# Query, key and value projections as three fp16 products of a split input, transposed by transfers

## The chip, the cores and the metric

The kernel runs on one NeuronCore of a Trainium2 chip. Its engines are TensorE (PE, matmuls, whose weight loads are listed as PEld), VectorE (DVE), ScalarE (ACT), GpSimd (POOL) and SyncE (SP, which here only issues transfers). The metric is the device time of one execution in microseconds (us); lower is better.

## The reference

Four layers with residuals over `x` of 32 items, 256 tokens, width 128: an attention with biases, a mixture of experts, an attention without biases, the mixture again. Cut to the part that matters:

```
x = x + attention_a(layernorm(x), Wq, bq, Wk, bk, Wv, bv, Wo)   # 16 heads of 8
x = x + ffn(layernorm(x), ...)
x = x + attention_b(layernorm(x), w_qkv, w_out)                  # 16 heads of 8
x = x + ffn(layernorm(x), ...)
# attention: q, k, v = xn @ Wq, xn @ Wk, xn @ Wv; softmax(q k^T) v; @ Wo
```

All of it is in fp32.

## The kernel before

The 32 items pass twice through one pipeline, once for each attention with the mixture behind it, as 64 turns. The program of each engine is a loop over steps n = -6 to 70 and, inside, over eight places p = 0 to 7; an engine does its instructions in exactly that order and waits for the others by semaphores. In step n TensorE works on several turns at once: the scores of turn n+2 for their maxima (`max_side`, L840, read by VectorE's `nmax`, L643), the scores of turn n again for the exponentials (`exp_side`, L850, read by ScalarE, L717), the weighted sums of turn n (`weigh`, L829), and at single places the small products of a turn's way in and out, which all go through one bank of PSUM, `m_bank`. `fill_m` lets each of these wait until the one before it has been read.

The way in of a turn is this. In step n VectorE takes the statistics of turn n+6. GpSimd normalises turn n+5 into `xy[.][:, 0]`, and turn n-3, behind its attention, into `xy[.][:, 1]` (L537). At p=6 TensorE transposes both, four 128x128 pieces (L1010), and ScalarE copies the first pair to `xnT` (L794) and the second to `normT` (L797). At p=2 of the next step the query and key projections read `xnT` (L816 from `by_columns`: eight fp32 matmuls of 32 columns of weights each; the trace counts two instructions for each fp32 matmul). ScalarE adds the biases and writes `qk32` (L753 and L754; in the second attention one copy, L756). GpSimd splits `qk32` into two fp16 parts (L550, L553), SP stores the parts to DRAM (`scratch`, six transfers, L431) and loads them back as `q_stack` and `k_stack` (L414) at its next step, once those stores have landed. At p=5 the value projection reads `xnT` too (L816), and ScalarE copies it to `values` (L781).

SP's order in a step is: wait for the stores of the step before to land, and for the exponentials' matmuls; issue the two loads; wait for `maxT` (the maxima, L724); issue its two transfers (L420); wait for the parts; issue the six stores. GpSimd's order is: the maxima (L515 to L519, which TensorE transposes at p=1, L950), the normalisation, the weights of the experts for one or two turns, the parts.

At p=3 TensorE transposes `oT` (L977), which shares `m_bank` and so waits until ScalarE has read the query and key product. After the query and key product at p=2 only one `exp_side`, one `max_side` and one more `exp_side` come before that.

In the opening, ScalarE and VectorE find the norms of the projections' weights and scale query and key weights against each other by powers of two, before the first projection.

Of the kernel before, what the change touches and what calls it, by code (L numbers as in the profile page):

```python
# [34 lines left out]
COARSE = 32768.0  # L35

# [25 lines left out]
def build(nc, x_dram_in, attn_w, attn_b, gate_w, down_w, down_b, up_w, up_b, tail_c, ident_c, iota_c, pick_c, out):  # L62
    ctx = ExitStack()
    with ctx:
# [19 lines left out]
        xnT = [sb(f"xnT{i}", [P, TOKENS]) for i in range(2)]  # L84
# [15 lines left out]
        bks = sb("bks", [P, 1])  # L100
        ident = sb("ident", [P, P])
        identh = sb("identh", [P, P], FP16)
        ones = sb("ones", [P, P])
        norms = sb("norms", [P, 4])
        norms_b = sb("norms_b", [P, 2])
        total = sb("total", [P, 2, 2])
        inverse = sb("inverse", [P, 2])
        ratio = sb("ratio", [P, 2])
        quarter = sb("quarter", [P, 2], U32)
        exponent = sb("exponent", [P, 2, 2], U32)  # L110
        factor = sb("factor", [P, 2, 2])
# [89 lines left out]
        def scalar_opening(act):  # L201
# [26 lines left out]
        def vector_opening(dve):  # L228
# [11 lines left out]
            dve.wait_ge(squares_done, 4)  # L240
            then(nc.vector.tensor_tensor(norms[:, 0:2], norms[:, 0:2], norms_b[:, :], ALU.add))
            assert done[0] == NORMS_READY
            dve.wait_ge(norms_summed, 1)
            then(nc.vector.tensor_scalar(total[:, :, :].rearrange("p a b -> p (a b)"), m_bank[:, 0:4], 1.0, 1e-30, ALU.mult, ALU.add))
            assert done[0] == TOTAL_READ
            then(nc.vector.reciprocal(inverse[:, :], total[:, :, 0]))
            then(nc.vector.tensor_tensor(ratio[:, :], total[:, :, 1], inverse[:, :], ALU.mult))
            then(nc.vector.tensor_scalar(quarter[:, :], ratio[:, :].bitcast(U32), 25, None, ALU.logical_shift_right))
            then(nc.vector.tensor_scalar(exponent[:, 0, :], quarter[:, :], 1.0, 96.0, ALU.mult, ALU.add))
            then(nc.vector.tensor_scalar(exponent[:, 1, :], quarter[:, :], -1.0, 158.0, ALU.mult, ALU.add))  # L250
            then(nc.vector.tensor_scalar(factor[:, :, :].bitcast(U32), exponent[:, :, :], 23, None, ALU.logical_shift_left))
            to_q, to_q_b = float(HEAD) ** -0.5, float(WIDTH) ** -0.5
            nc.vector.tensor_scalar(wa[:, 0:WIDTH], wa[:, 0:WIDTH], factor[:, 0, 0:1], to_q, ALU.mult, ALU.mult)
            nc.vector.tensor_scalar(wa[:, WIDTH:2 * WIDTH], wa[:, WIDTH:2 * WIDTH], factor[:, 1, 0:1], None, ALU.mult)
            nc.vector.tensor_scalar(bqs[:, :], wa[:, 4 * WIDTH:4 * WIDTH + 1], factor[:, 0, 0:1], to_q, ALU.mult, ALU.mult)
            nc.vector.tensor_scalar(bks[:, :], wa[:, 4 * WIDTH + 1:4 * WIDTH + 2], factor[:, 1, 0:1], None, ALU.mult)
            nc.vector.tensor_scalar(wb[:, 0:WIDTH], wb[:, 0:WIDTH], factor[:, 0, 1:2], to_q_b, ALU.mult, ALU.mult)
            nc.vector.tensor_scalar(wb[:, WIDTH:2 * WIDTH], wb[:, WIDTH:2 * WIDTH], factor[:, 1, 1:2], None, ALU.mult).then_inc(weights_ready, 1)  # L258
            dve.wait_ge(weights_ready, 1)

        def tensor_opening(pe):
            pe.wait_ge(balancing, NORMS_READY)
            nc.tensor.matmul(m_bank[:, 0:4], ones[:, :], norms[:, :], start=True, stop=True).then_inc(norms_summed, 1)
            m_reader[0] = (balancing, TOTAL_READ)
# [42 lines left out]
        def live(turn):  # L307

            return 0 <= turn < TURNS

        projections = [[w[:, i * WIDTH:(i + 1) * WIDTH] for i in range(4)] for w in (wa, wb)]
# [767 lines left out]
```

## Time and profile before

| | |
|---|---|
| time, median of 3 runs | 932.47 us (931.51 to 935.1) |
| the profiled execution: its own time | 931.88 us |
| its span, first to last instruction | 930.1 us |
| busy, PE | 861.5 us, 93% of the span |
| busy, DVE | 781.5 us, 84% |
| busy, ACT | 757.5 us, 81% |
| busy, POOL | 539.8 us, 58% |
| queue of SP: bytes, share of 16 transfer engines | 69.52 MB, 24.8% |

The profiled execution is 0.6 us below the median of the runs, and 1.8 us of it lie outside the span. The busy shares are means over an opening of about 50 us, a steady stretch to about 850 us and an ending.

### The profile page before, as it was taken

The page shows a single profiled execution, that of the slowest core. Times are in us where ns is not written, and L with a number is a line of the kernel's source. Part 1 is how long each engine was busy: PE and PEld are TensorE (multiplying, and loading weights), DVE is VectorE, ACT ScalarE, POOL GpSimd, SP SyncE. Part 2 cuts the span into 40 slices and gives each one's busy share as a digit, 9 for nine tenths or more (in the row PEclk, how much of TensorE's full clock was granted, in tenths as well). Part 3 has the DMA queues.
Part 4 walks back from the last instruction along what each step waited for, and adds up shares of the span by engine and source line. Part 5 has one row for each costly group of instructions (what it writes and reads, how often), then busy time and mean ns, then how long its engine had stood idle before and what let it go on. Part 6 is the DMA issues. An engine that isn't in the chain of part 4 may idle for free.

```text
span 930.1 us, 32135 instructions
## 1 busy us (share of the span) xinstructions
PE 861.5 (93%) x12592; PEld 444.0 (48%) x12592; DVE 781.5 (84%) x1410; ACT 757.5 (81%) x1305; POOL 539.8 (58%) x1086
## 2 busy tenths in 40 slices
PE   3699999999999999999999999999999999998875
PEld 1244444444445454455545445455554554554434
DVE  2889999999998989989898998989889888889533
ACT  2278888888888888888988898888898888897864
POOL 7345555545664766647565674657576485653432
PEclk9989999999999999999999999999999999999987
DMA  3354233222222222212222221222223133132001
GB/s 107 119 159 142 79 89 102 83 74 67 78 78 76 60 80 68 83 50 80 78 72 70 66 83 58 83 66 82 59 71 99 47 102 95 54 104 64 4 24 46
DMA packets 89862, 72.16 MB, mean 78 GB/s; under 512 B 5040, under 2 KB 72784, under 8 KB 89680
## 3 DMA queue, kind: packets, MB, share of 16 engines
q1 hardware_dynamic: 89280, 69.52, 24.8%
q8 instruction: 101, 1.65, 0.8%
q10 hardware_dynamic: 432, 0.59, 0.2%
q14 instruction: 49, 0.40, 0.1%
HBM read 39.68 MB, written 29.88 MB: 75 GB/s over the span
## 4 chain that ended last, share of the span: by engine, by line
PE 66%; DVE 18%; issue 8%; ACT 4%; POOL 2%; DMA 1%; POOLq 0%; SPq 0%; DVEq 0%; ACTq 0%
PE values_bank L829 19%; DVE nmax L643 14%; PE ring L840 11%; PE ring L850 10%; PE m_bank L816 9%; PE m_bank L977 4%; PE m_bank L1010 3%; PE ring L880 3%; PE ring L903 3%; ACT probs L717 2%; PE m_bank L950 1%; PE ring L895 1%; DMA wb<-in_attn_b 0%; DVE x L631 0%; DVE x L678 0%
## 5 line engine op out<-in xcount | busy, mean ns | idle before, releaser
L643 DVE TENSOR_REDUCE nmax<-ring 128x4 f32<-128x1024 f32 x512 | 603.7, 1216 | 46.6 <-PE ring L840 44.5
L717 ACT ACTIVATE probs<-ring 128x1024 f32<-128x1024 f32 x512 | 520.7, 1034 | 35.6 <-PE ring L850 32.9
L829 PE MATMUL values_bank<-probs,values 128*32 128x256 f32 x4096 | 277.0, 384 | 1.7 <-ACT probs L717 1.7
L850 PE MATMUL ring<-q_stack,k_stack 32*128 32x256 f16 x2048 | 198.4, 273 | 14.1 <-DVE nmax L643 14.0
L537 POOL TENSOR_SCALAR xy<-x,mv,rstd 128x128 f32<-128x128 f32 x256 | 201.7, 798 | 7.9
L840 PE MATMUL ring<-k_stack,q_stack 32*128 32x256 f16 x2048 | 183.2, 277 | 15.3 <-DMA k_stack<-scratch 5.1
L515 POOL TENSOR_SCALAR mparts<-nmax 128x32 f16<-128x32 f32 x64 | 14.1, 220 | 279.1 <-DVE nmax L643 279.0
L829 PEld LDWEIGHTS values_bank<-probs,values 128*32 128x32 f32 x4096 | 123.9, 109 | 63.8 <-issue 23.8
L850 PEld LDWEIGHTS ring<-q_stack,k_stack 32*128 32x128 f16 x2048 | 64.4, 92 | 132.7 <-issue 73.7
L840 PEld LDWEIGHTS ring<-k_stack,q_stack 32*128 32x128 f16 x2048 | 52.9, 93 | 115.4 <-ACT probs L717 41.2
L781 ACT COPY values<-m_bank 128x128 f32<-128x128 f32 x128 | 28.9, 278 | 60.3 <-PE m_bank L816 59.0
L553 POOL TENSOR_TENSOR parts<-qk,parts 128x512 f16<-128x512 f32 x64 | 74.3, 1160 | 5.3
L530 POOL TENSOR_TENSOR rstd<-varp,minus_half 128x4 f32<-128x4 f32 (+1 forms) x72 | 69.6, 967 | 6.0
L572 DVE BATCH_NORM_STATS2 raw<-x 128x6 f32<-128x128 f32 x256 | 60.9, 280 | 3.7 <-DMA x<-in_x 3.7
L631 DVE TENSOR_TENSOR x<-x,m_bank 128x256 f32<-128x256 f32 x64 | 27.0, 421 | 40.2 <-PE m_bank L816 40.2
L1010 PE MATMUL m_bank<-ident,xy 128*128 128x128 f32 x256 | 45.0, 294 | 5.4 <-ACT qk L754 1.0
L744 ACT COPY oT<-values_bank 128x512 f32<-128x512 f32 x64 | 37.6, 587 | 15.3 <-PE values_bank L829 15.3
L550 POOL TENSOR_SCALAR parts<-qk 128x512 f16<-128x512 f32 x64 | 39.7, 621 | 14.6 <-ACT qk L754 13.1
L678 DVE TENSOR_TENSOR x<-x,ring 128x512 f32<-128x512 f32 x32 | 22.0, 688 | 30.0 <-PE ring L903 30.0
L977 PE MATMUL m_bank<-ident,oT 128*128 128x128 f32 x256 | 41.9, 286 | 2.4 <-ACT oT L744 1.3
L816 PE MATMUL m_bank<-xnT,wa 128*32 128x256 f32 x512 | 38.6, 424 | 2.4 <-DVE wb L258 1.8
L482 POOL COPY wu<-up_sb 64x128 f32 x112 | 32.7, 292 | 11.8 <-POOL wd L476 9.1
(118 smaller groups left out, 959.7 us busy)
## 6 DMA issues: line engine op xcount, KB each, us to landing
scratch<-parts SPq DMA_DIRECT2D x384, 64.0 KB
q_stack<-scratch SPq DMA_DIRECT2D x64, 256.0 KB, 2.6
k_stack<-scratch SPq DMA_DIRECT2D x64, 256.0 KB, 3.0
out<-x SPq DMA_DIRECT2D x16, 256.0 KB, 3.0
x<-in_x SPq DMA_DIRECT2D x3, 768.0 KB, 6.5
q_stack<-maxT SPq DMA_DIRECT2D x128, 8.0 KB
x<-in_x SPq DMA_DIRECT2D x1, 896.0 KB, 6.7
x<-in_x SPq DMA_DIRECT2D x1, 640.0 KB, 5.3
```

Of the source, the lines that this page charges most:

```text
L530: nc.gpsimd.tensor_tensor(rstd[i][:, both, :], varp[i][:, both, :], minus_half[:, both, :], ALU.pow).then_inc(rstd_done, 1)
L537: last = nc.gpsimd.tensor_scalar(xy[i][:, m, t, :], x[:, (turn % ITEMS) * TILES + t, :], mv[i][:, m, t, 0:1], rstd[i][:, m, t:t + 1], ALU. ...
L553: nc.gpsimd.tensor_tensor(parts[i][:, 1], qk32[i][:, :, :], parts[i][:, 0], ALU.subtract).then_inc(parts_ready, 1)
L572: last = nc.vector.bn_stats(raw[i][:, t, :], x[:, (turn % ITEMS) * TILES + t, :])
L643: nc.vector.tensor_reduce(dst, src, axis=AX.X, op=ALU.max, negate=True).then_inc(max_done, 1)
L717: nc.scalar.activation(probs[g % 2][:, c:c + 2, :, :], pair_of("exps", n, p)[:, :, :].rearrange("p x (k q) -> p x k q", k=TILES), ACT.Exp) ...
L816: last = nc.tensor.matmul(out[at], stationary[:, at], moving, start=start, stop=stop, skip_group_check=True)
L829: last = nc.tensor.matmul(values_bank[32 * c:32 * (c + 1), a * TOKENS:(a + 1) * TOKENS], values[turn % RING][:, k, PER_GROUP * g + c, :], ...
L840: last = nc.tensor.matmul(pair_of("scores", turn, p)[:, a, t * TOKENS:(t + 1) * TOKENS], q_stack[z][rows, p // 2, t * P:(t + 1) * P], k_st ...
L850: last = nc.tensor.matmul(pair_of("exps", turn, p)[:, a, k * TOKENS:(k + 1) * TOKENS], k_stack[r][rows, of // 2, k * P:(k + 1) * P], q_sta ...
L977: last = nc.tensor.transpose(m_bank[:, at:at + P], oT[(n - 1) % 2][:, a, t * P:(t + 1) * P], ident[:, :])
L1010: last = nc.tensor.transpose(m_bank[:, at:at + P], xy[(n + 5) % 2][:, m, t, :], ident[:, :])
```

## The change

GpSimd writes the normalised turn n+5, scaled up by 2^8, as two fp16 parts into `xn` (a rounding and a rest, two more instructions). SP transposes them by four transfers of 128x128 into `xnT`, which now has four buffers of two fp16 parts each, at a place between the transfers of `maxT` and the stores of the parts. TensorE no longer transposes that half of `xy`, and ScalarE no longer copies it. The weights are split once, in the opening, into two fp16 parts (`w_parts`), after scaling by powers of two that now cover the value weights and their output weights too. Query, key and value projections become three fp16 products each (`PRODUCTS`: first by first, first by second, second by first part), with weights of 128 columns: per turn, query and key take 6 matmuls of 256 columns, and value 6 of 128, in place of 8 and 8 of `by_columns`. ScalarE undoes the scaling by a `scale` of its copies. The output projection stays as it was.

```diff
+PRODUCTS = ((0, 0), (0, 1), (1, 0))
...
-        xnT = [sb(f"xnT{i}", [P, TOKENS]) for i in range(2)]
+        xn = [sb(f"xn{i}", [P, 2, TILES, WIDTH], FP16) for i in range(2)]
+        xnT = [sb(f"xnT{i}", [P, 2, TOKENS], FP16) for i in range(RING)]
+        w_parts = [sb(f"w_parts{i}", [P, 2, 3 * WIDTH], FP16) for i in range(2)]
...
-            for c, w in enumerate((wa[:, 0:WIDTH], wa[:, WIDTH:2 * WIDTH], wb[:, 0:WIDTH], wb[:, WIDTH:2 * WIDTH])):
-                last = nc.scalar.activation(onT[:, 0:WIDTH], w, ACT.Square, scale=float(WIDTH) ** 0.5, accum_out=norms[:, c:c + 1])
+            for c, w in enumerate(m[:, i * WIDTH:(i + 1) * WIDTH] for m in (wa, wb) for i in range(3)):
+                last = nc.scalar.activation(onT[:, 0:WIDTH], w, ACT.Square, scale=float(WIDTH) ** 0.5, accum_out=norms[:, c // 3, c % 3:c % 3 + 1])
...
+            to_q = (float(HEAD) ** -0.5, float(WIDTH) ** -0.5)
+            for b, w in enumerate((wa, wb)):
+                nc.vector.tensor_scalar(w[:, 0:WIDTH], w[:, 0:WIDTH], factor[:, b, 0:1], to_q[b], ALU.mult, ALU.mult)
+                for i in (1, 2):
+                    last = nc.vector.tensor_scalar(w[:, i * WIDTH:(i + 1) * WIDTH], w[:, i * WIDTH:(i + 1) * WIDTH], factor[:, b, i:i + 1], None, ALU.mult)
+                if b == 0:
+                    nc.vector.tensor_scalar(bqs[:, :], wa[:, 4 * WIDTH:4 * WIDTH + 1], factor[:, 0, BIAS_Q:BIAS_Q + 1], to_q[0], ALU.mult, ALU.mult)
+                    nc.vector.tensor_scalar(bks[:, :], wa[:, 4 * WIDTH + 1:4 * WIDTH + 2], factor[:, 0, BIAS_K:BIAS_K + 1], None, ALU.mult)
+                    nc.vector.tensor_scalar(bvs[:, :], wa[:, 4 * WIDTH + 2:4 * WIDTH + 3], factor[:, 0, BIAS_V:BIAS_V + 1], None, ALU.mult)
+                then(nc.vector.tensor_scalar(w[:, 3 * WIDTH:4 * WIDTH], w[:, 3 * WIDTH:4 * WIDTH], factor[:, b, BACK_V:BACK_V + 1], None, ALU.mult))
+                then(nc.vector.tensor_copy(w_parts[b][:, 0, :], w[:, 0:3 * WIDTH]))
+                nc.vector.tensor_tensor(w_parts[b][:, 1, :], w[:, 0:3 * WIDTH], w_parts[b][:, 0, :], ALU.subtract).then_inc(weights_ready, 1)
+                dve.wait_ge(weights_ready, b + 1)
...
+                    if live(n + 5):
+
+                        sp.wait_ge(xn_ready, (n + 5) + 1)
+                        if live(n + 1):
+                            sp.wait_ge(v_done, (n + 1) + 1)
+                        for part in range(2):
+                            for t in range(TILES):
+                                sp.dma_start(xnT[(n + 5) % RING][:, part, t * P:(t + 1) * P], xn[(n + 5) % 2][:, part, t, :],
+                                             transpose=True).then_inc(xnT_in[(n + 5) % 2], 16)
...
-                        if norm_steps(n) > 2:
-                            pool.wait_ge(xyT_done, norm_steps(n - 2))
+                        if live(n - 5):
+                            pool.wait_ge(yT_done, (n - 5) + 1)
                         for m, turn in ((0, n + 5), (1, n - 3)):
                             for t in range(TILES):
                                 if live(turn):
                                     last = nc.gpsimd.tensor_scalar(xy[i][:, m, t, :], x[:, (turn % ITEMS) * TILES + t, :], mv[i][:, m, t, 0:1],
                                                                    rstd[i][:, m, t:t + 1], ALU.subtract, ALU.mult)
                         last.then_inc(xy_ready, 1)
+                        if live(n + 5):
+                            if live(n + 3):
+                                pool.wait_ge(xnT_in[(n + 3) % 2], (n + 3) // 2 * 64 + 64)
+                            pool.wait_ge(xy_ready, norm_steps(n))
+                            nc.gpsimd.tensor_scalar(xn[i][:, 0, :, :], xy[i][:, 0, :, :], 1.0, 0.0, ALU.mult, ALU.add).then_inc(xhi_done, 1)
+                            pool.wait_ge(xhi_done, (n + 5) + 1)
+                            nc.gpsimd.tensor_tensor(xn[i][:, 1, :, :], xy[i][:, 0, :, :], xn[i][:, 0, :, :], ALU.subtract).then_inc(xn_ready, 1)
...
+                        same = factor[:, (n + 4) // ITEMS, SAME:SAME + 1]
                         if n + 4 < ITEMS:
-                            nc.scalar.activation(qk32[i][:, 0, :], src[:, 0, :], ACT.Identity, bias=bqs[:, :])
-                            last = nc.scalar.activation(qk32[i][:, 1, :], src[:, 1, :], ACT.Identity, bias=bks[:, :])
+                            nc.scalar.activation(qk32[i][:, 0, :], src[:, 0, :], ACT.Identity, bias=bqs[:, :], scale=same)
+                            last = nc.scalar.activation(qk32[i][:, 1, :], src[:, 1, :], ACT.Identity, bias=bks[:, :], scale=same)
                         else:
-                            last = nc.scalar.copy(qk32[i][:, :, :], src)
+                            last = nc.scalar.activation(qk32[i][:, :, :], src, ACT.Copy, scale=same)
                         last.then_inc(qk32_ready, 1)
...
-                    if p == 5 and (live(n + 5) or live(n - 3)):
-                        act.wait_ge(xyT_done, norm_steps(n))
-                        if live(n + 5):
-                            nc.scalar.copy(xnT[(n + 5) % 2][:, :], m_bank[:, 0:TOKENS]).then_inc(xnT_ready, 1)
-                        if live(n - 3):
-                            item = (n - 3) % ITEMS
-                            nc.scalar.activation(normT[:, item:item + 1, :], m_bank[:, TOKENS:2 * TOKENS].unsqueeze(1), ACT.Copy,
-                                                 accum_out=pooled[:, item:item + 1]).then_inc(yT_ready, 1)
+                    if p == 5 and live(n - 3):
+                        act.wait_ge(yT_done, (n - 3) + 1)
+                        item = (n - 3) % ITEMS
+                        nc.scalar.activation(normT[:, item:item + 1, :], m_bank[:, 0:TOKENS].unsqueeze(1), ACT.Copy, scale=2.0 ** -UP,
+                                             accum_out=pooled[:, item:item + 1]).then_inc(yT_ready, 1)
...
-                        wq, wk = projections[(n + 4) // ITEMS][0:2]
+                        parts_w, parts_x = w_parts[(n + 4) // ITEMS], xnT[(n + 4) % RING]
                         fill_m(pe, qk32_ready, (n + 4) + 1)
-                        if n + 4 == 0:
-                            pe.wait_ge(weights_ready, 1)
-                        pe.wait_ge(xnT_ready, (n + 4) + 1)
-                        for a, wmat in enumerate((wq, wk)):
-                            last = by_columns(m_bank[:, a * TOKENS:(a + 1) * TOKENS], wmat, xnT[(n + 4) % 2][:, :],
-                                              start=(a == 0), stop=(a == 1))
+                        if n + 4 in (0, ITEMS):
+                            pe.wait_ge(weights_ready, (n + 4) // ITEMS + 1)
+                        pe.wait_ge(xnT_in[(n + 4) % 2], (n + 4) // 2 * 64 + 64)
+                        for a in range(2):
+                            for k, (w, h) in enumerate(PRODUCTS):
+                                last = nc.tensor.matmul(m_bank[:, a * TOKENS:(a + 1) * TOKENS], parts_w[:, w, a * WIDTH:(a + 1) * WIDTH], parts_x[:, h, :],
+                                                        start=(a == 0 and k == 0), stop=(a == 1 and k == len(PRODUCTS) - 1), skip_group_check=True)
                         last.then_inc(qk_done, 1)
...
-                        wv = projections[(n + 3) // ITEMS][2]
+                        parts_w, parts_x = w_parts[(n + 3) // ITEMS], xnT[(n + 3) % RING]
                         fill_m(pe, v_ready, (n + 3) + 1)
                         for t in range(TILES):
-                            last = by_columns(m_bank[:, t * P:(t + 1) * P], xnT[(n + 3) % 2][:, t * P:(t + 1) * P], wv,
-                                              start=(t == 0), stop=(t == TILES - 1))
+                            for k, (w, h) in enumerate(PRODUCTS):
+                                last = nc.tensor.matmul(m_bank[:, t * P:(t + 1) * P], parts_x[:, h, t * P:(t + 1) * P], parts_w[:, w, 2 * WIDTH:3 * WIDTH],
+                                                        start=(t == 0 and k == 0), stop=(t == TILES - 1 and k == len(PRODUCTS) - 1), skip_group_check=True)
                         last.then_inc(v_done, 1)
...
-                    if p == 6 and (live(n + 5) or live(n - 3)):
-                        fill_m(pe, *((yT_ready, (n - 3) + 1) if live(n - 3) else (xnT_ready, (n + 5) + 1)))
+                    if p == 6 and live(n - 3):
+                        fill_m(pe, yT_ready, (n - 3) + 1)
                         pe.wait_ge(xy_ready, norm_steps(n))
-                        for m in range(0 if live(n + 5) else 1, 2 if live(n - 3) else 1):
-                            for t in range(TILES):
-                                at = (m * TILES + t) * P
-                                last = nc.tensor.transpose(m_bank[:, at:at + P], xy[(n + 5) % 2][:, m, t, :], ident[:, :])
-                        last.then_inc(xyT_done, 1)
+                        for t in range(TILES):
+                            last = nc.tensor.transpose(m_bank[:, t * P:(t + 1) * P], xy[(n + 5) % 2][:, 1, t, :], ident[:, :])
+                        last.then_inc(yT_done, 1)
```

On SP, in a plain step of the first attention, the row of transfers before was this (the names in brackets are the semaphores that an issue waits for: `bounced` the stores' landing, `t_done` the exponentials' matmuls, `hi_ready` and `parts_ready` the two parts of `qk32`).

```order
L414 DMA q_stack<-scratch 128x1024 [waits t_done,bounced1]
L414 DMA k_stack<-scratch 128x1024
L420 DMA q_stack<-maxT 4x4x256 [waits maxT_ready]
L420 DMA q_stack<-maxT 4x4x256
L431 DMA scratch<-parts 4x32x256 [waits hi_ready,stack_in0]
L431 DMA scratch<-parts 4x32x256 x3
L431 DMA scratch<-parts 4x32x256 [waits parts_ready]
L431 DMA scratch<-parts 4x32x256
```

Now it is this, at the same place.

```order
L433 DMA q_stack<-scratch 128x1024 [waits t_done,bounced0]
L433 DMA k_stack<-scratch 128x1024
L439 DMA q_stack<-maxT 4x4x256 [waits maxT_ready]
L439 DMA q_stack<-maxT 4x4x256
L447 DMA_TRANSPOSE xnT<-xn 128x128 [waits v_done,xn_ready]
L447 DMA_TRANSPOSE xnT<-xn 128x128 x3
L459 DMA scratch<-parts 4x32x256 [waits hi_ready,stack_in1]
L459 DMA scratch<-parts 4x32x256 x3
L459 DMA scratch<-parts 4x32x256 [waits parts_ready]
L459 DMA scratch<-parts 4x32x256
```

Four transposing transfers and a wait for `xn_ready` stand ahead of the stores; nothing else moved.

On PE, from the query and key product (p=2) to the transposes of `oT` (p=3), a plain step before reads so.

```order
L816 MATMUL m_bank<-xnT,wa 32x256 x8
L850 MATMUL ring<-q_stack,k_stack 128x256 x4
L840 MATMUL ring<-k_stack,q_stack 128x256 x4
L850 MATMUL ring<-q_stack,k_stack 128x256 x4
L977 MATMUL m_bank<-ident,oT 128x128 x4
```

Now:

```order
L998 MATMUL m_bank<-xnT,w_parts 128x256 x6
L883 MATMUL ring<-q_stack,k_stack 128x256 x4
L873 MATMUL ring<-k_stack,q_stack 128x256 x4
L883 MATMUL ring<-q_stack,k_stack 128x256 x4
L1011 MATMUL m_bank<-ident,oT 128x128 x4
```

Six fp16 matmuls stand for eight fp32 ones; what follows is the same.

On PE at p=5 and p=6, from the value product to the transposes of `xy`, before:

```order
L816 MATMUL m_bank<-wa,xnT 32x128 x8
L829 MATMUL values_bank<-probs,values 32x256 x8
L1000 MATMUL m_bank<-ident,o 128x128 x2
L850 MATMUL ring<-q_stack,k_stack 128x256 x4
L840 MATMUL ring<-k_stack,q_stack 128x256 x4
L1010 MATMUL m_bank<-ident,xy 128x128 x4
```

and now:

```order
L1024 MATMUL m_bank<-w_parts,xnT 128x128 x6
L862 MATMUL values_bank<-probs,values 32x256 x8
L1035 MATMUL m_bank<-ident,o 128x128 x2
L883 MATMUL ring<-q_stack,k_stack 128x256 x4
L873 MATMUL ring<-k_stack,q_stack 128x256 x4
L1043 MATMUL m_bank<-ident,xy 128x128 x2
```

Two of the four transposes are gone, and the value product has six matmuls.

## Rows read from the trace of the kernel before

**Rows 1.** Windows, steady stretch: busy us (count) of PE, PEld, DVE, ACT, POOL; clock; DMA share; GB/s.

```profile
50.00:850.00 800.00, 774.88 (x11682) 398.43 (x11676) 714.43 (x1249) 692.25 (x1178) 481.97 (x947) 1.00 0.27 80
```

**Rows 2.** Chain that ended last, 560 to 586 us, second attention: start, us, what.

```profile
561.93 0.22 PE ring L895 x2
...
574.46 1.23 DVE nmax L643
...
576.12 0.59 PE m_bank L1010 x4
...
581.38 1.00 PE m_bank L816 x16
```

**Rows 3.** The same chain, 300 to 326 us, first attention.

```profile
313.57 0.30 ACT oT L744
...
315.33 0.49 ACT qk L754
...
315.87 0.66 PE m_bank L977 x4
```

**Rows 4.** Timeline of SP's issues, 300 to 328 us: start, us, line, transfer, count.

```profile
306.62 3.44 SPq L431 DMA_DIRECT2D scratch<-parts  x6
312.87 0.33 SPq L414 DMA_DIRECT2D q_stack<-scratch  x1
...
313.72 1.16 SPq L420 DMA_DIRECT2D q_stack<-maxT  x2
318.50 3.46 SPq L431 DMA_DIRECT2D scratch<-parts  x6
324.89 0.33 SPq L414 DMA_DIRECT2D q_stack<-scratch  x1
```

**Rows 5.** Timeline of PE, 564 to 590 us: start, us, line, tiles, shapes, count.

```profile
573.42 0.64 PE L816 MATMUL m_bank<-wb,xnT 128*32 128x128 f32 x16
573.88 1.05 PE L829 MATMUL values_bank<-probs,values 128*32 128x256 f32 x16
574.86 0.44 PE L1000 MATMUL m_bank<-ident,o 128*128 128x128 f32 x2
575.23 0.39 PE L850 MATMUL ring<-q_stack,k_stack 32*128 32x256 f16 x4
575.73 0.39 PE L840 MATMUL ring<-k_stack,q_stack 32*128 32x256 f16 x4
...
583.33 0.66 PE L977 MATMUL m_bank<-ident,oT 128*128 128x128 f32 x4
```

**Rows 6.** Timeline of ACT, 564 to 590 us.

```profile
582.53 0.59 ACT L756 COPY qk<-m_bank 128x512 f32<-128x512 f32 x1
```

**Rows 7.** The page's costliest groups: the split of `qk32` on POOL, mean ns after the comma.

```profile
L553 POOL TENSOR_TENSOR parts<-qk,parts 128x512 f16<-128x512 f32 x64 | 74.3, 1160 | 5.3
...
L550 POOL TENSOR_SCALAR parts<-qk 128x512 f16<-128x512 f32 x64 | 39.7, 621 | 14.6 <-ACT qk L754 13.1
```

**Rows 8.** Timeline of POOL, a step's first instruction; in brackets its idle time before.

```profile
180.10 0.22 POOL L515 TENSOR_SCALAR mparts<-nmax 128x32 f16<-128x32 f32 x1 [4.89 <-DVE nmax L643]
431.32 0.22 POOL L515 TENSOR_SCALAR mparts<-nmax 128x32 f16<-128x32 f32 x1 [1.40 <-DVE nmax L643]
443.41 0.22 POOL L515 TENSOR_SCALAR mparts<-nmax 128x32 f16<-128x32 f32 x1 [3.13 <-DVE nmax L643]
...
756.66 0.22 POOL L515 TENSOR_SCALAR mparts<-nmax 128x32 f16<-128x32 f32 x1
```

**Rows 9.** Chain that ended last, the opening.

```profile
5.97 0.41 ACT onT L208 x2
...
11.12 0.23 DVE wb L258
...
11.45 1.97 PE m_bank L816 x16
```

**Rows 10.** Timeline of PE, 300 to 328 us: the next step's query and key product.

```profile
325.99 1.07 PE L816 MATMUL m_bank<-xnT,wa 128*32 128x256 f32 x16
```

More of the change, by code:

```diff
@@ L103, in build @@
         ones = sb("ones", [P, P])
-        norms = sb("norms", [P, 4])
+        norms = sb("norms", [P, 2, 3])
         norms_b = sb("norms_b", [P, 2])
[L106 to L111, printed above, removed]
+        total = sb("total", [P, 2, 3])
+        quarter = sb("quarter", [P, 2, 3], U32)
+        level = sb("level", [P, 2, 3])
+        both_of = sb("both_of", [P, 2, 2])
+        exponent = sb("exponent", [P, 2, 8], U32)
+        factor = sb("factor", [P, 2, 8])
         minus_half = sb("minus_half", [P, 2, TILES])
@@ L245, in vector_opening @@
             assert done[0] == TOTAL_READ
[L246 to L250, printed above, removed]
@@ L256, in vector_opening @@
[L256 to L259, printed above, removed]
+            then(nc.vector.tensor_scalar(quarter[:, :, :], total[:, :, :].bitcast(U32), 25, None, ALU.logical_shift_right))
@@ new lines, in vector_opening @@
+            then(nc.vector.tensor_scalar(level[:, :, :], quarter[:, :, :], 1.0, 0.0, ALU.mult, ALU.add))
+            nc.vector.tensor_tensor(both_of[:, :, 0], level[:, :, 0], level[:, :, 1], ALU.add)
+            then(nc.vector.tensor_tensor(both_of[:, :, 1], level[:, :, 1], level[:, :, 0], ALU.subtract))
+            bias = 127.0
+            nc.vector.tensor_scalar(exponent[:, :, 0:3], level[:, :, :], -2.0, bias + TO_TARGET, ALU.mult, ALU.add)
+            nc.vector.tensor_scalar(exponent[:, :, SAME], both_of[:, :, 0], 1.0, bias - UP - TO_TARGET, ALU.mult, ALU.add)
@@ new lines, in vector_opening @@
+            nc.vector.tensor_scalar(exponent[:, :, BIAS_Q], both_of[:, :, 1], 1.0, bias, ALU.mult, ALU.add)
+            nc.vector.tensor_scalar(exponent[:, :, BIAS_K], both_of[:, :, 1], -1.0, bias, ALU.mult, ALU.add)
+            nc.vector.tensor_scalar(exponent[:, :, BIAS_V], level[:, :, 2], -2.0, bias + UP + TO_TARGET, ALU.mult, ALU.add)
+            then(nc.vector.tensor_scalar(exponent[:, :, BACK_V], level[:, :, 2], 2.0, bias - UP - TO_TARGET, ALU.mult, ALU.add))
+            then(nc.vector.tensor_scalar(factor[:, :, :].bitcast(U32), exponent[:, :, :], 23, None, ALU.logical_shift_left))
@@ L261, in tensor_opening @@
         def tensor_opening(pe):
             pe.wait_ge(balancing, NORMS_READY)
[L263 removed]
+            nc.tensor.matmul(m_bank[:, 0:6], ones[:, :], norms[:, :, :].rearrange("p a b -> p (a b)"), start=True, stop=True).then_inc(norms_summed, 1)
             m_reader[0] = (balancing, TOTAL_READ)
@@ L309, in live @@
             return 0 <= turn < TURNS
-        projections = [[w[:, i * WIDTH:(i + 1) * WIDTH] for i in range(4)] for w in (wa, wb)]
+        out_weights = [w[:, 3 * WIDTH:4 * WIDTH] for w in (wa, wb)]
         raw_done, raw2_done, mv_done, mv2_done = sem("raw_done"), sem("raw2_done"), sem("mv_done"), sem("mv2_done")
         var_done, rstd_done, xy_ready = sem("var_done"), sem("rstd_done"), sem("xy_ready")
-        xyT_done, xnT_ready, yT_ready = sem("xyT_done"), sem("xnT_ready"), sem("yT_ready")
+        xhi_done, xn_ready = sem("xhi_done"), sem("xn_ready")
+        xnT_in = [sem(f"xnT_in{i}") for i in range(2)]
+        yT_done, yT_ready = sem("yT_done"), sem("yT_ready")
         qk_done, qk32_ready = sem("qk_done"), sem("qk32_ready")
@@ L786, in step @@
                         if n - 1 < ITEMS:
-                            last = nc.scalar.activation(onT[:, :], m_bank[:, 0:TOKENS], ACT.Identity, bias=wa[:, 514:515])
+                            last = nc.scalar.activation(onT[:, :], m_bank[:, 0:TOKENS], ACT.Identity, bias=bvs[:, :])
                         else:
```

17 lines of the change are left out of this document (8 added, 9 removed).

## The prediction

> **What bounds the kernel now.** I read the busy time of the steady stretch first, then the chain that ended last inside one step of each attention, and then the queue that the change loads, SP's. From 50 to 850 us TensorE is busy 774.88 of 800 us at full granted clock (1.00), VectorE 714.43, ScalarE 692.25 and GpSimd 481.97 [rows 1]. So TensorE is the bound, but VectorE and ScalarE are within 8% and 11% of it, and a gain on TensorE soon meets one of them. The chain shows where. In a step of the second attention it runs through TensorE except for one stretch: a maximum of 1.23 us on VectorE that ends where TensorE goes on towards the transposes of `xy`, whose four pieces cost 0.59 us there; the query and key product costs 1.00 us [rows 2]. In the first attention it leaves TensorE a second time: from 313.57 it runs through ScalarE (the copy of `oT`, an exponential, the two biased copies of `qk32`, the last from 315.33 for 0.49 us) and returns at 315.87 with the transposes of `oT` [rows 3]. There TensorE waits for ScalarE, so a shorter product ahead of it wins nothing.
>
> SP works in a closed loop, since its first wait in a step is for the stores of the step before to land. The six stores take 3.46 us to issue, end at 321.96, and the loads start at 324.89, 2.93 us later; from the first load to `maxT` it is 0.85 us, and `maxT` takes 1.16 us [rows 4]. That is 3.46 + 2.93 + 0.85 + 1.16 = 8.40 us which SP needs for a step, whatever the others do.
>
> **The change, part by part: TensorE.** Two of four transposes at p=6 go. Two such pieces elsewhere (L1000) take 575.23 - 574.86 = 0.37 us from start to start [rows 5], four 0.59 [rows 2], so 0.22 us is saved, on the chain in both attentions. (Both ends: 0.15, if the first pieces carry most of the cost, and half, 0.30.) The steps that do this under a busy TensorE are n = 0 to 58: 59 x 0.22 = 13.0 us.
>
> Query and key become six 16-bit matmuls of 256 columns. A pair of such matmuls (L895, bf16) costs 0.22 us on the chain [rows 2], so six cost 0.66 against 1.00: 0.34 us less. In the first attention I count none of it, as ScalarE ends last there [rows 3]. In the second, ScalarE's copy ends at 582.53 + 0.59 = 583.12 [rows 6] and the transposes of `oT` start at 583.33 [rows 5], so 0.21 us can be won before ScalarE ends last there too: 32 x 0.21 = 6.7 us. The ends are 0 and 0.34.
>
> The value product takes 573.88 - 573.42 = 0.46 us; then TensorE reaches an `exp_side` of four at 575.23, which takes 0.39 us, and the next `max_side` starts only at 575.73 [rows 5], when VectorE releases it [rows 2]. Six matmuls of 128 columns cost between half of 0.11 each (0.33 us) and all of it (0.66). A gain is lost in that wait of 0.11 us; a loss of 0.20 would pass it by 0.09, 5 us over 59 steps. I count zero.
>
> **ScalarE and GpSimd.** ScalarE loses the copy to `xnT`, which is on neither chain: zero. GpSimd gains two instructions of 256 columns. Their kinds at 512 columns take 0.62 and 1.16 us [rows 7]; halves are 0.31 and 0.58, the whole is the other end; with a fixed part and the gaps I take 1.2 us a step (0.9 to 1.8). GpSimd idles 3.13 us before the first instruction of a plain step (4.89 early on); a plain step is 443.41 - 431.32 = 12.09 us [rows 8]. A step shorter by 0.43 and work longer by 1.2 leave 1.5 us. That cover is thin where GpSimd splits the experts' biases, 1.40 us at 431.32, and gone where it has also prepared two turns, at 756.66 [rows 8]. There the maxima's parts come late, behind them their transposes at p=1, and all of TensorE behind these. The batches' table gives seven such splits up to n = 58: six times 0.2 and once 1.6 are 2.8 us, of which I take 2, as TensorE asks a little after the parts are due (0 to 8).
>
> **Opening.** Before the first product ScalarE squares six weights in place of four, 0.43 us each (0.41 and the gap); VectorE does about five more scalings of numbers and four more of weights or biases at some 0.2 us (the last one before took 0.23), less two that now come later, and two splits of 384 columns, an estimated 0.45 each; the first product, 1.97 us at the opening's clock, becomes some 0.45 shorter [rows 9]. That is 0.86 + 1.0 + 0.4 + 0.9 - 0.45, about 2.5 us later for all that follows (0 to 5).
>
> **SP and the four transfers.** They must fit twice. First, into the loop: a step of 12.09 - 0.43 = 11.66 us leaves 11.66 - 8.40 = 3.26 us, or 0.82 us for each; at (12.09 - 8.40) / 4 = 0.92 us the loop alone makes a step as long as before. No row shows a transposing transfer. Issues cost SP from 0.33 us (one load) to 0.58 (`maxT` 1.16 / 2, a store 3.46 / 6) [rows 4]; the far end is 2.93 us, if each had to land before the next. I take 0.58: `maxT` is the row that also goes from SBUF to SBUF. 4 x 0.58 = 2.3 us fit, with 1 us to spare. Second, by the time of use: GpSimd finishes `xn` before the parts, whose first store goes out at 318.50; so it is ready by 318.50 + 1.2 - 0.62 = 319.1, issued by 321.4, landed (2.93) by 324.3, and the product that reads it starts at 325.99 [rows 4, 10], or 0.43 earlier: 1.3 us to spare. What is queued behind them on SP are the stores, whose loads are wanted only a step later. So the transfers cost zero, as long as an issue stays under 0.82 us.
>
> Here the Trainium skill speaks against the change: the page "VectorE: DVE Perf Modes", section "The three transpose paths", gives 390 ns for a 128x128 piece of 2-byte elements on TensorE and 1309 ns by a transfer, and advises TensorE where PSUM will do as the destination. No run so far shows it. If 1.31 us were what a piece holds SP, the loop would be 8.40 + 5.24 = 13.6 us and the time, an estimate from that page, 931.9 + 59 x 1.55 + 2.5 = 1026 us.
>
> **Sum.** 13.0 + 6.7 - 2.0 - 2.5 = 15.2 us less than the profiled execution's 931.9: 916.7. The median of the runs lies 0.6 above that execution, so 917 us.
>
> **Rivals.** (a) *SP's queue becomes the bound*, the other sign. It decides from 0.92 us an issue. For it: the loop has only 3.7 us of room, a transposing issue is a different instruction, and the skill's page above points that way. Against it: no issue of a comparable shape takes over 0.58. At twice the price of a store, 1.15 us, the loop is 13.0 us, 0.91 over 12.09. 59 x 0.91 + 2.5 gives 988 us, less where steps with an expert group are longer and leave room. At 2.93 us an issue the loop would be 20.1 us.
>
> (b) *The gain turns into waits*: VectorE (89% busy) and ScalarE (87%) [rows 1] hold TensorE up at other places of the step, and a third of the 19.7 us remains, 6.5, against 2.5 in the opening and GpSimd's 2.8 in full: 931 us, no change. For it speaks rows 3; against it, that the chain of the second attention has only one such stretch.
>
> (c) *The transfers land late, with SP free*: if the transfer engines serve the four one after another at 2.93 us each, the last lands at 319.1 + 11.7 = 330.8, 5.2 us after 325.6. A late product returns by way of the maxima and GpSimd's next normalisation two steps later, so 2.6 us a step, 59 times: 1088 us. Against it: the transfer engines are busy 27% of the time [rows 1].
>
> **How the numbers follow.** My forecast has a chance of 0.50, (a) 0.28, (b) 0.13, (c) 0.09. What a measurement tells from no change here is about 0.5%, 4.7 us. The forecast's own range is 908 (0.30 and 0.34 saved, little lost) to 927, nine tenths of it faster by over 0.5%: 0.45; with a fifth of (b), 0.48 faster. The rest of (b) and the forecast's last tenth give 0.14 within; (a) and (c) 0.38 slower once a little is kept for the edges. The range runs from 908, below which I leave 0.05, to 1000, above which lie most of (c) and the dearer quarter of (a), 0.15.
>
> **What would show it.** Right: SP still waits for the parts each step and each of its transposing issues lasts 0.8 us or less; TensorE has no wait for a transfer at the query and key product; plain steps shorter by about 0.2 us in the first and 0.4 in the second attention; `oT`'s transposes waiting for ScalarE in both. Wrong by (a): no wait of SP for the parts, steps of the length of its loop, long issues. By (c): TensorE idle ahead of the product, released by a transfer. By (b): the transposes and the product shorter as said, steps still 12.1 us. By GpSimd: the first instruction of its step without idle time in plain steps.

## The result

The changed kernel takes 1018.4 us (median of 4 runs, 1017.3 to 1020.2) against 933.3 us for the kernel before on the same chip: ratio 1.091, 95% interval 1.089 to 1.094. That is slower, above the range, and on the side of rival (a). The profiled execution has a span of 1017.5 us.

The page of the changed kernel, busy time and the shares of the chain that ended last:

```profile
PE 854.2 (84%) x11184; PEld 439.9 (43%) x11184; DVE 792.1 (78%) x1424; ACT 752.2 (74%) x1245; POOL 606.6 (60%) x1214
...
SPq 42%; PE 18%; DMA 16%; DVE 8%; POOL 6%; issue 6%; ACT 3%; POOLq 1%; DVEq 0%; ACTq 0%
```

Only GpSimd is busier than before as a share of its time, and the chain no longer lies on TensorE: SP's queue has 42% of it and the landing of transfers 16%. In the steady stretch, the row that answers to [rows 1] has TensorE busy 701 of 800 us in place of 775, all engines down but GpSimd:

```profile
50.00:850.00 800.00, 701.01 (x9390) 355.61 (x9388) 656.63 (x1130) 620.19 (x1007) 495.68 (x965) 0.96 0.29 83
```

SP's timeline of the changed kernel, the same stretch as [rows 4] (start, us, line, transfer, count):

```profile
303.25 3.45 SPq L459 DMA_DIRECT2D scratch<-parts  x6
309.91 0.34 SPq L433 DMA_DIRECT2D q_stack<-scratch  x1
...
310.76 1.17 SPq L439 DMA_DIRECT2D q_stack<-maxT  x2
312.04 5.96 SPq L447 DMA_TRANSPOSE xnT<-xn  x4
318.10 3.46 SPq L459 DMA_DIRECT2D scratch<-parts  x6
324.96 0.34 SPq L433 DMA_DIRECT2D q_stack<-scratch  x1
...
327.09 4.95 SPq L447 DMA_TRANSPOSE xnT<-xn  x4
```

Four transposing issues hold SP for 4.95 to 5.96 us; the old issues cost what they cost before. The stores start the moment the transposes are issued, and the next loads start when the stores have landed: from load to load it is 324.96 - 309.91 = 15.05 us, where a plain step was 12.1. SP's waits and the duration of one transposing issue (minimum, median, maximum in ns):

```profile
SPq L433 <- DMA scratch<-parts: 161.4, 61, 3.6
...
SPq L447 <- POOL xn L574: 14.0, 10, 5.2
```

```profile
L447 SPq DMA_TRANSPOSE xnT<-xn x256: 1094/1232/2417, 9.6 to 913.8; - x128
```

SP's long wait is the landing of its own stores; for GpSimd it hardly waits (14.0 us in all), and for TensorE 3.7 us in all. So it is a loop that SP alone closes. What TensorE sees of it is a wait at the query and key product, and then a second price:

```profile
PE m_bank L998 <- DMA xnT<-xn: 67.3, 35, 6.4
```

Windows of the changed kernel (columns as in [rows 1]; the number behind the counts is the granted clock):

```profile
316.00:319.20 3.20, 0.57 (x13) 0.13 (x8) 2.53 (x4) 1.63 (x3) 3.09 (x5) 0.99 0.06 11
319.20:325.00 5.80, 5.60 (x46) 2.71 (x48) 2.05 (x5) 2.85 (x4) 4.27 (x10) 0.50 0.24 69
```

TensorE had been busy 0.57 of 3.2 us, and was then granted half its clock (1.2 GHz) for the next 5.8 us. The product, 0.75 us from start to start at 304.49, took 1.37 us there.

### The profile page after: what moved, and what is told of

It reads as the page before. It is cut to its first block, busy times and chain, and to the rows that moved or that the text cites. A ratio compares the mean times of both kernels' runs of the same rounds, so it can differ in the third digit from the quotient of the medians.

```text
span 1017.5 us, 29763 instructions
## 1 busy us (share of the span) xinstructions
PE 854.2 (84%) x11184; PEld 439.9 (43%) x11184; DVE 792.1 (78%) x1424; ACT 752.2 (74%) x1245; POOL 606.6 (60%) x1214
## 4 chain that ended last, share of the span: by engine, by line
SPq 42%; PE 18%; DMA 16%; DVE 8%; POOL 6%; issue 6%; ACT 3%; POOLq 1%; DVEq 0%; ACTq 0%
SPq L447 23%; DMA scratch<-parts 14%; SPq L459 11%; PE values_bank L862 5%; DVE nmax L678 5%; SPq L439 4%; SPq L433 4%; POOL xy L565 2%; PE ring L913 2%; PE ring L936 2%; ACT probs L752 2%; PE ring L873 2%; PE ring L883 2%; PE m_bank L1011 1%; DMA xnT<-xn 1%
## 5 line engine op out<-in xcount | busy, mean ns | idle before, releaser
L862 PE MATMUL values_bank<-probs,values 128*32 128x256 f32 x4096 | 289.4, 397 | 1.7 <-ACT probs L752 1.7
L873 PE MATMUL ring<-k_stack,q_stack 32*128 32x256 f16 x2048 | 186.4, 285 | 32.9 <-DMA k_stack<-scratch 15.2
L883 PE MATMUL ring<-q_stack,k_stack 32*128 32x256 f16 x2048 | 199.8, 280 | 14.6 <-DVE nmax L678 13.5
L543 POOL TENSOR_SCALAR mparts<-nmax 128x32 f16<-128x32 f32 x64 | 13.8, 216 | 249.1 <-DVE nmax L678 248.5
L862 PEld LDWEIGHTS values_bank<-probs,values 128*32 128x32 f32 x4096 | 121.8, 112 | 76.0 <-issue 27.1
L883 PEld LDWEIGHTS ring<-q_stack,k_stack 32*128 32x128 f16 x2048 | 68.7, 94 | 120.7 <-issue 63.0
L998 PE MATMUL m_bank<-xnT,w_parts 128*128 128x256 f16 x384 | 60.6, 301 | 67.4 <-DMA xnT<-xn 67.3
L998 PEld LDWEIGHTS m_bank<-xnT,w_parts 128*128 128x128 f16 x384 | 35.5, 104 | 89.0 <-issue 77.0
L1011 PE MATMUL m_bank<-ident,oT 128*128 128x128 f32 x256 | 48.1, 318 | 12.3 <-ACT qk L790 8.9
L789 ACT ACTIVATE qk<-m_bank,bqs,factor 128x256 f32<-128x256 f32 x32 | 18.1, 565 | 54.0 <-PE m_bank L998 54.0
L504 POOL COPY wd<-down_sb 128x64 f32 x128 | 25.8, 236 | 36.3 <-issue 36.3
```

Of the source, the lines that this page charges most:

```text
L862: last = nc.tensor.matmul(values_bank[32 * c:32 * (c + 1), a * TOKENS:(a + 1) * TOKENS], values[turn % RING][:, k, PER_GROUP * g + c, :], ...
L873: last = nc.tensor.matmul(pair_of("scores", turn, p)[:, a, t * TOKENS:(t + 1) * TOKENS], q_stack[z][rows, p // 2, t * P:(t + 1) * P], k_st ...
L883: last = nc.tensor.matmul(pair_of("exps", turn, p)[:, a, k * TOKENS:(k + 1) * TOKENS], k_stack[r][rows, of // 2, k * P:(k + 1) * P], q_sta ...
L998: last = nc.tensor.matmul(m_bank[:, a * TOKENS:(a + 1) * TOKENS], parts_w[:, w, a * WIDTH:(a + 1) * WIDTH], parts_x[:, h, :], start=(a == ...
```

## The experiments

Two theories stood first. **A**: the issue of a transposing transfer costs SP 1.23 us, and the loop of SP's issues sets the step (A2: the price goes by the piece of 128 columns, not by the instruction). **B**: moving or landing the data is what is slow, whatever SP issues. C to H came from the first traces and are told where they are tried. "Kernel 4" is the kernel of experiment 4. Line numbers differ a little from kernel to kernel; the names stay.

**1. One transfer in place of four**, over all 512 columns.

```diff
-for part in range(2):
-    for t in range(TILES):
-        sp.dma_start(xnT[..][:, part, t*P:(t+1)*P], xn[..][:, part, t, :], transpose=True)
+sp.dma_start(xnT[..].rearrange("p a (t c) -> p (a t) c", c=P),
+             xn[..].rearrange("p a t w -> p (a t w)"), transpose=True)
```

> One transposing transfer of 512 columns per turn stands for the four of 128; data, order and waits stay. Theory A, SP's loop is the bound and an issue has its price per instruction: one issue of about 1.2 to 1.7 us takes some 3.5 us from SP's loop, the loop falls below TensorE's 11.7 to 12.1 us a step, about 920 us. A2, the price goes by the pieces moved: issue of about 4.5 to 5 us, about 1010 us. Theory B, the transfers' data phase is late for TensorE: the same data, no change, about 1018 us.

948.4 us (944.0 to 950.4), ratio 1.014, interval 1.010 to 1.018. Its transposing issues and SP's waits:

```profile
L445 SPq DMA_TRANSPOSE xnT<-xn x64: 1201/1228/2557, 9.5 to 837.2; - x64
```

```profile
SPq L445 <- POOL xn L573: 108.5, 55, 5.2
SPq L454 <- POOL parts L584: 75.7, 42, 4.5
```

One issue of four times the data costs the same 1.23 us, so the price is the instruction's, and A2 and B fall. SP waits for GpSimd again. But A had expected 920, and 28 us of that did not come.

**2. Only the first parts transposed**, two transfers a step; the products read the first part where they should read the second, so the rest of `x` is left out. GpSimd still makes both parts.

```diff
-for part in range(2):
+for part in range(1):
...
-parts_x[:, h, :]
+parts_x[:, 0, :]
```

> Only the first parts are transposed, by two transfers; the products with the rest read the first part instead, so the rest of x is left out of the result, with the same number of matmuls and the same work on GpSimd. Theory A: 2 x 1.23 us less in SP's loop, 13.9 to 11.4 us, so TensorE is the bound again, about 925 us, with qk steps 0.2 to 0.4 us under those of before. Theory B: half the wait of TensorE remains, about 970 us. If GpSimd's two more instructions were the cause, no change, 1018 us.

948.4 us (947.0 to 951.4), 1.016 (1.012 to 1.019): halving the issues does the same as merging them, and here too A's 925 is missed, by 23 us.

**3. The transfers of `maxT` ahead of SP's wait for the landing**, four transposes as in the change, and **4. the same with one transfer**.

```diff
 def step(sp, n, p):
+    if live(n + 1):   # wait for maxT_ready, its two transfers
+        ...
     if live(n + 3):   # wait for the landing, two loads
         ...
-    if live(n + 1):
-        ...
     if live(n + 5):   # the transposing transfers
```

> On SP the two transfers of maxT stand ahead of the wait for the stores' landing instead of behind the loads; the four transposing transfers are untouched. Theory A: their 1.2 us fall into the wait for the landing, the loop is 1.2 us shorter in some 55 steps, about 955 us. Theory B (transfers land late by themselves): no change, 1018 us.

> One transfer per turn and maxT ahead of the landing, both. Theory A: 920 us as with one transfer alone, since TensorE is the bound already; with A2 (price by pieces) about 950 us. Theory B: 1018 us.

977.7 us (974.5 to 980.0), 1.046 (1.042 to 1.050), and 946.0 us (944.6 to 946.6), 1.013 (1.010 to 1.016). The third takes work out of the loop without touching the transposing transfers and wins 41 us, which a loop of issues explains and B does not; A had expected 955, 23 us less than measured. The fourth wins 2 us over the first, within the spread of their runs, so SP no longer sets the end there; 920 was missed again.

**5. The transfers alone**: the kernel before, with four transposing transfers a step from a constant tile to tiles that nobody reads.

```diff
+for part in range(2):
+    for t in range(TILES):
+        sp.dma_start(extraT[(n+5) % RING][:, part, t*P:(t+1)*P], extra[:, part, t, :], transpose=True)
```

> The kernel of before with four transposing transfers a step added to SP's queue at the same place, from a constant tile to tiles nobody reads; everything else as before. Theory A: the queue alone makes the loss. Its loop becomes 8.4 + 4 x 1.23 = 13.3 us or a little more, so 1.2 to 1.9 us a step over 12.1: 1000 to 1040 us. Rival F: the transfers cost nothing by themselves and the loss comes from the other edits: 933 us.

1004.1 us (1000.5 to 1010.6), 1.072 (1.069 to 1.076). Nothing else was changed, and 69 us of the loss are there. SP's timeline of this kernel (its traced execution took 1010.6 us, the longest of the four):

```profile
303.85 3.46 SPq L445 DMA_DIRECT2D scratch<-parts  x6
310.46 0.34 SPq L418 DMA_DIRECT2D q_stack<-scratch  x1
...
312.53 4.96 SPq L433 DMA_TRANSPOSE extraT<-extra  x4
317.60 3.96 SPq L445 DMA_DIRECT2D scratch<-parts  x6
324.23 0.34 SPq L418 DMA_DIRECT2D q_stack<-scratch  x1
```

The loop is 324.23 - 310.46 = 13.8 us in this step; the stores end at 321.56, so their landing takes 2.7 us of it (3.2 us in the step before).

**6. The parts transposed on TensorE**: no transposing transfer; four 16-bit transposes at p=6, and ScalarE copies them to `xnT`.

```diff
+for k in range(2 * TILES):
+    nc.tensor.transpose(m_bank.bitcast(FP16)[:, 2*TOKENS + k*P : ...], xn[..][:, k // TILES, k % TILES, :], identh)
...
+nc.scalar.copy(xnT[..], m_bank.bitcast(FP16)[:, 2*TOKENS:4*TOKENS])
```

> The changed kernel with its two parts transposed on TensorE (four 16-bit transposes and one copy by ScalarE to xnT) and no transposing transfer. Theory A with C: SP's loop is as short as before, and what is left are the opening (3 us), GpSimd's longer work at the end (8 us), and some 0.2 us more on TensorE a step, of which the shorter product gives back about as much: 935 to 955 us, near 945. Rival F: something in the three-product form itself costs the bulk, not the queue: over 980 us.

944.7 us (943.3 to 946.6), 1.010 (1.008 to 1.013). So F falls, and without SP's loop and without any transposing transfer the three products are still no gain, though TensorE and ScalarE do these transposes here. Where the remainder lies is read from the start of ScalarE's copy to `maxT`, one a turn (us, in the traces):

| kernel | turn 2 | turn 29 | turn 53 | turn 61 |
|---|---|---|---|---|
| before | 59.36 | 408.49 | 733.56 | 847.57 |
| changed | 72.67 | 465.51 | 812.83 | 934.08 |
| 5, transfers alone | 70.35 | 462.45 | 806.27 | 924.35 |
| 4, one transfer, `maxT` first | 61.72 | 414.40 | 739.73 | 861.66 |
| 8, register loads earlier | 60.31 | 412.86 | 738.15 | 856.46 |
| 9, half copy | 60.69 | 408.46 | 732.59 | 851.68 |
| 10, before with half copy | 58.98 | 406.13 | 730.53 | 843.70 |

Kernel 4 is 2.4 us late at turn 2, 5.9 at turn 29, 6.2 at turn 53 and 14.1 at turn 61. So of what the queue left, 2.4 us come in the opening, 3.5 in the first attention, 0.3 in the second up to turn 53, and 8 behind it. Two theories follow, C for the gain that is missing (TensorE's shorter work only meets other waits, ScalarE's first) and D for the end (GpSimd's register loads).

**7. The removed transposes put back into kernel 4**, as work whose result nobody reads.

> The kernel with one transposing transfer a step and maxT ahead, with the two transposes on TensorE that the change took out put back as work whose result nobody reads. Theory C: the 0.22 us they took was never won, since without them eight short matmuls (the last exp_side and max_side before the third weigh) run one behind the other in 0.65 us where they ran beside each other in 0.43 us, the second side being released by ScalarE's exponential: then the time stays within 3 us of the 946 us without them and the step of the second attention stays 12.04 us. Rival: the 0.22 us was won at each of 59 steps and something else took it back: then the time rises by some 13 us to 959 us.

945.6 us (942.6 to 948.8), 1.011 (1.008 to 1.013), as without them: taking them out won nothing. TensorE's timeline in the second attention shows why, kernel 8 first, then kernel 6 with its six transposes:

```profile
592.21 0.39 PE L875 MATMUL ring<-k_stack,q_stack 32*128 32x256 f16 x4
592.53 0.44 PE L1045 MATMUL m_bank<-ident,xy 128*128 128x128 f32 x2
592.90 0.39 PE L885 MATMUL ring<-q_stack,k_stack 32*128 32x256 f16 x4
593.22 0.39 PE L875 MATMUL ring<-k_stack,q_stack 32*128 32x256 f16 x4
593.54 1.07 PE L864 MATMUL values_bank<-probs,values 128*32 128x256 f32 x16
```

```profile
593.26 0.44 PE L1040 MATMUL m_bank<-ident,xy 128*128 128x128 f32 x2
593.54 0.39 PE L1048 MATMUL m_bank<-identh,xn 128*128 128x128 f16 x4
593.86 0.28 PE L879 MATMUL ring<-q_stack,k_stack 32*128 32x256 f16 x2
593.96 0.28 PE L869 MATMUL ring<-k_stack,q_stack 32*128 32x256 f16 x2
593.98 0.27 PE L879 MATMUL ring<-q_stack,k_stack 32*128 32x256 f16 x2
594.08 0.27 PE L869 MATMUL ring<-k_stack,q_stack 32*128 32x256 f16 x2
594.28 1.07 PE L858 MATMUL values_bank<-probs,values 128*32 128x256 f32 x16
```

From the first transpose to `weigh` (L864, L858) it is 593.54 - 592.53 = 1.01 us with two transposes and 594.28 - 593.26 = 1.02 with six. After six, the eight matmuls of the two sides run beside each other (0.42 us); after two they run one behind the other (0.64 us), since the second side's bank is not free earlier. In the kernel before it was 0.59 + 0.43 on the chain, and with the removed transposes put back it is so again, in kernel 7's chain:

```profile
593.13 0.59 PE m_bank L1044 x4
593.71 0.21 PE ring L882 x2
...
594.14 1.00 PE values_bank L861 x16
```

In the first attention little more was won: 1.07 us (155.03 to 156.10) in kernel 8 in place of 1.12 (152.91 to 154.03) in the kernel before. That ScalarE's exponential is what frees the bank is my reading of the ring's order and was not tried.

**8. GpSimd's loads of the experts' numbers into registers ahead of the split**, in kernel 4.

```diff
 last.then_inc(xy_ready, 1)
+for turn in PREPARED.get(n, ()):
+    if turn // GROUP not in experts:
+        experts[turn // GROUP] = experts_of(turn // GROUP, pool)
 if live(n + 5):   # waits for xy, then the split
```

> The kernel with one transposing transfer a step and maxT ahead, with GpSimd's loads of the experts' numbers into registers issued behind the normalisation and ahead of the split into two parts (the order of before). Theory D: the 8 us lost between turns 53 and 60 are in good part the 1.9 us that these loads now cost GpSimd by themselves, three times in that stretch where it has no idle time: 940 to 943 us, and the idle time of 1.9 us ahead of the copies to wd gone. Rival E: the split's own 1.2 us a step is what makes GpSimd late there: 946 us, no change.

942.9 us (940.7 to 945.1), 1.009 (1.006 to 1.011): 3 us faster as the medians go, with intervals that overlap kernel 4's. The traces carry it. GpSimd in kernel 4, then the same place in kernel 8 (in brackets the idle time before):

```profile
744.58 0.67 POOL L573 TENSOR_TENSOR xn<-xy,xn 128x256 f16<-128x256 f32 x1
747.12 0.41 POOL L503 COPY wd<-down_sb 128x64 f32 x2 [1.87 <-issue]
```

```profile
742.99 0.67 POOL L576 TENSOR_TENSOR xn<-xy,xn 128x256 f16<-128x256 f32 x1
743.60 0.41 POOL L503 COPY wd<-down_sb 128x64 f32 x2
```

The 1.87 us are gone, and between turns 53 and 61 kernel 8 falls behind by 4.3 us in place of 7.9. So D held for about half of the end; E, the split's own time, is left for the other half and was not tried by itself.

**9 and 10. ScalarE's copy of `oT` halved**, in kernel 8 and in the kernel before (half of the attention's result is left out).

```diff
-nc.scalar.copy(oT[..][:, :, :], values_bank.rearrange("p (a q) -> p a q", a=SHARES))
+nc.scalar.copy(oT[..][:, 0, :], values_bank[:, 0:TOKENS])
```

> The kernel with one transposing transfer, maxT ahead and the register loads ahead of the split, with ScalarE's copy of oT cut to half its columns (256 of 512; the other half is a constant, so half of the attention's result is left out). The copy becomes some 0.25 us shorter at the place where, by theory C, TensorE now waits for ScalarE (0.23 us a step ahead of the scores in the second attention, and through both biased copies in the first). Theory C: the gain of the shorter product comes free, 0.2 us at some 57 steps: 928 to 934 us. Rival G: what holds TensorE there is the loop through VectorE's maxima or the scores' three banks, and ScalarE only ends last by a little: 941 to 943 us, no change.

> The kernel of before with the same cut of ScalarE's copy of oT to half its columns (half of the attention's result is left out). Theory C: TensorE's longer product of 1.00 us covers ScalarE there in the second attention and all but 0.03 us in the first, so a shorter copy wins at most some 3 us: 930 to 935 us. Rival H: ScalarE holds this kernel up as much as the other one: some 924 us, 10 us faster.

937.0 us (934.3 to 940.6), 1.003 (1.001 to 1.004), and 929.4 us (927.1 to 931.6), 0.995 (0.993 to 0.997). Both miss: the copy is worth 5 to 6 us in either kernel, so as a whole it does not tell C from H. By stretches it does. From turn 2 to 29 kernel 8 loses 3.4 us on the kernel before and kernel 9 gains 1.4, a swing of 4.8 against 2.0 in the kernel before: in the first attention ScalarE held back the gain. (These are single traces; the loss of that stretch is 3.4 to 3.7 us in those of experiments 2, 4, 6, 7 and 8, and 4.7 in that of 1, so 4.8 is no scatter.) From turn 29 to 53 the swing is 1.2 and 0.7, near nothing: there it is G. In that stretch of kernel 8 TensorE waits for ScalarE behind the shorter product:

```profile
587.14 0.39 PE L875 MATMUL ring<-k_stack,q_stack 32*128 32x256 f16 x4 [0.23 <-ACT probs L754]
```

Such waits of `max_side` for ScalarE are 17.2 us in the whole of kernel 8 and 2.4 in the kernel before. But taking them away opens nothing. Kernel 9's chain in the second attention:

```profile
578.69 3.50 DVE nmax L682 x3
...
588.40 1.00 PE values_bank L866 x16
589.40 0.32 PE ring L887 x4
589.73 0.62 PE m_bank L853 x16
...
590.37 0.33 DVE x L670
...
590.74 3.50 DVE nmax L682 x3
594.24 0.04 issue
594.28 0.39 PE ring L887 x4
```

With ScalarE out of the way the chain goes through three maxima of VectorE, and the step from maxima to maxima is still 590.74 - 578.69 = 12.05 us. In the kernel before this second route was already there, VectorE first, then TensorE:

```profile
579.47 3.49 DVE L643 TENSOR_REDUCE nmax<-ring 128x4 f32<-128x1024 f32 x3
```

```profile
583.01 0.39 PE L850 MATMUL ring<-q_stack,k_stack 32*128 32x256 f16 x4
```

The maxima end at 582.96, and TensorE starts the exponentials' matmuls at 583.01: the room in which a shorter product could win anything was at most 0.05 us, and kernel 9 starts 0.04 us behind the maxima (594.24 to 594.28) where it does wait for them.

## Why the prediction was wrong, step by step

**The step that failed** is "I take 0.58: `maxT` is the row that also goes from SBUF to SBUF". A transposing issue holds SP for 1.23 us, past the break-even of 0.92 that the working had named. The bounds, 0.33 to 2.93, did hold it; the choice between them went by the kind of memory at both ends, and the kind of instruction was what mattered. The Trainium skill, "VectorE: DVE Perf Modes", section "The three transpose paths", had 1309 ns for a 128x128 piece of 2-byte elements by a transfer, without saying what it is the time of. The trace has 1232 ns, 6% less, for the time that the queue is held, 2.4 us to the landing, and experiment 1 adds that four pieces in one instruction cost no more. The estimate by that page, 1026 us, was nearest.

**Rival (a)** came true, dearer than its 988 us. Its loop at 1.15 us was 13.0; measured alone, in the step of experiment 5 shown, it is 13.8, and 14.4 on average from turn 2 to 53: some issues take longer than their median, so that four take 4.9 to 6.2 us (median 5.4) in place of 4.6. The changed kernel takes 14.5 us a turn in either stretch of the table, the kernel before 12.9 from turn 2 to 29 and 13.5 from 29 to 53, where more of its steps are longer ones with an expert group. So the loss is 1.62 and 0.93 us a turn (1.59 and 0.78 with the transfers alone), and that the second is (a)'s 0.91 is luck: loop and step are both longer than (a)'s 13.0 and 12.09. Another 13.3 us are lost by turn 2 already (11.0 with the transfers alone), where (a) counted 2.5 for the opening. Whether TensorE's low clock after its waits adds to the loss was not taken apart. Rival (c) is not confirmed: transfers land 2.4 us after issue, and TensorE's 67 us of waiting for them come from SP's lateness, since they go to nothing with one transfer, where the landing is the same.

**The gains on TensorE** were right as pieces and wrong as gains. The transposes are 0.37 us in place of 0.59 (592.53 to 592.90), the product is 0.75 us (forecast 0.66, before 1.00), the value product 0.44 (counted as no change). Of 13.0 + 6.7 us forecast, none arrived: 13.0 became lost overlap, 6.7 met VectorE's maxima in the second attention. That is rival (b) in kind, though hidden in the changed kernel behind (a); its counter-argument, "the chain of the second attention has only one such stretch", was the wrong reading: a chain shows which wait ended last, not by how much, and the other route ended 0.05 us earlier. In the first attention ScalarE ended last, as [rows 3] had it.

**ScalarE** was put at zero, for the copy that it loses. But its copies to `qk32` now also scale by a number read from a tile, and the two biased ones lie on the very chain of [rows 3]. The first of them, before and in the changed kernel (mean ns behind the comma):

```profile
L753 ACT ACTIVATE qk<-m_bank,bqs 128x256 f32<-128x256 f32 x32 | 15.3, 477 | 15.4 <-PE m_bank L816 15.3
```

```profile
L789 ACT ACTIVATE qk<-m_bank,bqs,factor 128x256 f32<-128x256 f32 x32 | 18.1, 565 | 54.0 <-PE m_bank L998 54.0
```

The second goes from 482 to 562 ns. In a plain step of the first attention the way from ScalarE's copy of `oT` to the transposes of `oT` is 2.48 us in kernel 8 (147.79 to 150.27) and 2.30 in the kernel before (145.86 to 148.16), 0.18 us more. Less the 0.05 us won at p=6 this makes 0.13 us a step, and a plain step there is indeed 12.38 us in place of 12.25 (from `maxT` to `maxT`, 147.25 to 159.63 and 145.32 to 157.57); over 27 turns that is the 3.4 us which this attention loses. The scaling was not taken away by itself.

**GpSimd's** instructions were sized right (0.41 + 0.67 us and the gaps, 1.3; forecast 1.2). Their cost was not: 2 forecast, 8 measured at the end of kernel 4, at the top of the bounds. Unforeseen was that the wait between normalisation and split keeps GpSimd from loading registers while it computes, 1.87 us more ahead of a group. **The opening** cost 2.4 us in kernel 4, where 2.5 was forecast, but 1.0 to 1.5 us in kernels 7, 8 and 9, so the match is in part luck; the two splits of weights, estimated at 0.45 us each, took 0.36 and 0.64.

With one transfer and `maxT` first, then, the loss falls from 85 to 13 us; with the registers it is 8, and no version here that computes the whole result beats the kernel before.

## What to carry to other kernels

Before adding transfers to a queue, write its loop down with the landing in it, and price each new kind of instruction at its dear end if the trace has no row for it: here the sign hung on that one number, and the remedy, one instruction for four pieces, was cheap. A gain is worth the room to the second-latest wait at the same place, so read the time at which each releaser of the instruction ended, not only the last. A semaphore wait put between two pieces of an engine's work can also stop what its sequencer did ahead under the first piece (1.87 us here). And an instruction that gets one more operand is to be priced anew, also where it seems to stay as it was.

## What the runs showed of the hardware that was not expected

A transposing transfer costs its queue 1.23 us per instruction, 128 or 512 columns alike (1232 and 1228 ns), where plain issues cost 0.34 to 0.56; it lands 2.4 us after its issue, the plain loads after 2.6 and 2.9. Two sides of four short matmuls ran beside each other in 0.42 us or one behind the other in 0.64 us; that the release of the second side decides it is a reading. ScalarE's biased copy of 256 columns took 0.08 to 0.09 us longer once it also scaled by a number from a tile (477 to 565 ns). And after 3.2 us with TensorE mostly waiting, 5.8 us at half the clock followed.
